# A graph network's count products: some of them moved from the tail into the gather phase

## The reference

```python
def _L0_gnn_ref(feat, weight, src, dst, etypes):
    h_src = feat[src]
    for r in range(num_rels):
        mask = etypes == r
        msg = msg + h_src * mask[:, None].astype(feat.dtype) @ weight[r]
    return jax.ops.segment_sum(msg, dst, num_segments=feat.shape[0])

def _L1_gnn_ref(x, edge_index, edge_attr, W_l, b_l, W_r, W_e, b_e):
    agg = jax.ops.segment_sum(x[row], col, num_segments=N)
    cnt = jax.ops.segment_sum(jnp.ones(...), col, num_segments=N)
    mean = agg / jnp.maximum(cnt, 1.0)[:, None]
    out = mean @ W_l + b_l + x @ W_r
    e = edge_attr @ W_e + b_e
    return out + jnp.zeros_like(out).at[col].set(e)

h = jnp.maximum(_layernorm(x), 0.0)
x = x + _L0_gnn_ref(h, L0_gnn_weight, src, dst, edge_type_16)
h = jnp.maximum(_layernorm(x), 0.0)
x = x + _L1_gnn_ref(h, edge_index, edge_attr_16, ...)
```

## Time and profile before

| | |
|---|---|
| median of three runs | 4880.84 us |
| profiled execution | 4871.31 us, span 4869.5 us |
| mean granted clock of TensorE | 0.807 |
| busy: PE, DVE, ACT, POOL | 2981.7, 3515.4, 1431.9, 3123.5 us |
| DMA | 575.14 MB, 118 GB/s over the span |

### The profile page before, as it was taken

One profiled execution on the slowest core, in us unless ns is written; L12 is line 12 of the kernel. 1 busy time (PEld: TensorE's weight loads), 2 busy tenths in 40 slices (PEclk: granted clock), 3 DMA queues, 4 the chain that ended last, 5 costly groups with the idle time before them and its releaser, 6 DMA issues.

```text
span 4869.5 us, 76484 instructions
## 1 busy us (share of the span) xinstructions
PE 2981.7 (61%) x23324; PEld 2583.8 (53%) x23325; DVE 3515.4 (72%) x17837; ACT 1431.9 (29%) x2462; POOL 3123.5 (64%) x3190
## 2 busy tenths in 40 slices
PE   1554555555555555656565565656666666669999
PEld 0224444444444544545455555555555555559999
DVE  4656788788788878888788888878877887871012
ACT  0332333333333333333333333333333333330000
POOL 1037777777777777777777777777777777770000
PEclk9975766667777777777788788888888888889999
DMA  9862333333333232223222222222222221127999
GB/s 98 300 243 85 112 106 116 104 101 99 102 109 93 85 98 90 79 82 92 81 76 68 68 70 67 67 61 62 59 55 53 50 51 45 45 78 317 408 387 365
DMA packets 257987, 575.14 MB, mean 118 GB/s; under 512 B 117787, under 2 KB 163931, under 8 KB 235323
## 3 DMA queue, kind: packets, MB, share of 16 engines
q1 hardware_dynamic: 78182, 443.67, 23.9%
q0 software_dynamic: 101568, 105.81, 11.0%
q10 hardware_dynamic: 77842, 20.86, 3.3%
HBM read 334.10 MB, written 248.81 MB: 120 GB/s over the span
## 4 chain that ended last, share of the span: by engine, by line
POOL 61%; issue 20%; PE 13%; DMA 3%; DVE 1%; ACTq 1%; ACT 1%; POOLq 0%; DVEq 0%; SPq 0%
POOL msg L413 60%; PE ps L1040 9%; PE ps L948 2%; DMA msg<-rel_table,istage 1%; DMA edge_ends<-arena 1%; POOL wrel L650 1%; ACTq L764 1%; PE ps L421 1%; DVE onehot L1145 1%; ACT arena L802 0%; DMA arena<-in_dst 0%; DVE arena L606 0%; PE ps L1024 0%; PE ps L974 0%; PE ps L958 0%
## 5 line engine op out<-in xcount | busy, mean ns | idle before, releaser
L413 POOL DMA_INDIRECT msg<-rel_table,istage x3125 | 3060.3, 979 | 954.1 <-issue 949.5
L802 ACT CAST arena<-ps 128x784 bf16<-128x784 f32 x1568 | 1245.6, 835 | 2647.5 <-PE ps L974 2634.9
L421 PE MATMUL ps<-onehot,msg 128*81 128x128 f32 x6250 | 1134.6, 347 | 1391.5 <-DMA msg<-rel_table,istage 1203.9
L421 PEld LDWEIGHTS ps<-onehot,msg 128*81 128x81 f32 x6250 | 962.9, 198 | 1515.5 <-DMA msg<-rel_table,istage 1305.8
L1285 DVE TENSOR_SCALAR batch<-iota_h,wrel 128x196 bf16<-128x196 bf16 x4312 | 1243.3, 293 | 0.0
L1284 DVE TENSOR_SCALAR batch<-iota_h,wrel 128x128 bf16<-128x128 bf16 x4312 | 1173.6, 275 | 13.7 <-PE ps L974 13.6
L974 PE MATMUL ps<-batch 128*128 128x196 bf16 x4312 | 673.1, 299 | 172.4 <-DVE batch L1285 97.6
L439 DVE TENSOR_SCALAR onehot<-iota_w,arena 128x128 f32<-128x128 f32 x3125 | 677.5, 295 | 0.0
L974 PEld LDWEIGHTS ps<-batch 128*128 128x128 bf16 x4312 | 473.3, 119 | 280.0 <-DVE batch L1285 148.5
L1285 DVE TENSOR_SCALAR arena<-iota_h,wrel 128x196 bf16<-128x196 bf16 x1960 | 564.0, 291 | 0.0
L1284 DVE TENSOR_SCALAR arena<-iota_h,wrel 128x128 bf16<-128x128 bf16 x1960 | 532.7, 275 | 10.9 <-PE ps L974 10.0
(11 more groups left out here) (147 smaller groups left out, 1116.3 us busy)
## 6 DMA issues: line engine op xcount, KB each, us to landing
arena<-counts SPq DMA_DIRECT2D x66, 1568.0 KB, 9.5
rel_table<-arena SPq DMA_DIRECT2D x98, 512.0 KB, 3.6
msg<-rel_table,istage POOLq DMA_INDIRECT x3125
counts<-arena SPq DMA_DIRECT2D x10, 3136.0 KB, 9.8
attr<-in_edge_attr SPq DMA_DIRECT2D x125, 200.0 KB
arena<-counts SPq DMA_DIRECT2D x18, 1344.0 KB, 14.4
counts<-arena SPq DMA_DIRECT2D x8, 2688.0 KB, 9.1
counts<-arena SPq DMA_DIRECT2D x7, 2912.0 KB, 9.7
```

Source lines behind the costliest of these rows:

```text
L413: pool.indirect_dma_start(msg[:, k, 0:D], None, table, bass.IndirectOffsetOnAxis(ap=istage[:, k:k + 1].bitcast(U32), axis=0)).then_inc(got ...
L421: mm = pe.matmul(ps[0:rows, bank, 0:WIN], msg[:, k, 0:rows], onehot[:, k, :], start=(k == 0), stop=(k == K - 1))
L802: nc.scalar.copy(cblk[:, h, :, u * WU * WD:(u + 1) * WU * WD].rearrange("p t (w d) -> p w t d", d=WD), unit_cols(u).rearrange("p w (t d) - ...
```

## The change

**Products of stored counts in the gather phase.** A planner now gives each slot up to 26 count products (EACH). Besides the early ones there are 148 late ones ("mults" that are not early), 3122 matmuls: as soon as more batches of `y` are final, SP reloads pieces of up to 7 source blocks of a stored count block into six rooms, three slots ahead (`load_room`), PE multiplies them (`mult_slot`), and DVE reduces the bank and adds it to `x_sb` (`mult_result`). The rooms lie over the index arrays of the first 36 superblocks, so this starts at slot 183. The tail keeps what is left, 2366 matmuls in 106 pieces instead of 5488 in 154, in five PSUM banks.

**Units of one bank.** WU goes from 4 to 2, so a unit's two products fill one PSUM bank; three banks take turns where two pairs did, and two banks are for the count products.

**Attribute product.** ACT makes it with five activations a group (`attr_group`) instead of one tensor_tensor on DVE.

```diff
-WU = 4
+WU = 2
+WINS = 16
...
-    RUNS_AT, KEY_STEPS = 8, 9
+    RUNS_AT, KEY_STEPS = 16, 9
+    RING, UNIT_BANKS = WINS // WU, (2, 3, 4)
...
+    EACH, MOST_TILES, ROOM_TILES, STORE_SLOTS, LOAD_SLOTS = 26, 28, TB, 4, 3
+    ROOMS, ROOM_SB = 6, -(-ROOM_TILES * P // K)
+    for c in range(LAST):
+        left = EACH
+        while left:
+            if not mults or mults[-1]["at"] == mults[-1]["t1"]:
...
+                    known = sum(mid_at[n]["done"] <= c for n in range(NB)) * TB
+                    least = 3 * TB if c < SLOTS - 65 else 2 * TB if c < SLOTS - 20 else TB
+                    can = [b for b in range(HEAD_WHOLE, NT) if c >= full_at[b] + STORE_SLOTS + LOAD_SLOTS
+                           and c > mid_at[b // TB]["split"] and (b < first_early or b in early_mult)
+                           and known - done[b] >= least]
...
+            mults_at[c].append((len(mults) - 1, m["at"], m["at"] + n))
...
-        def unit_cols(u):
-
-            q = 2 + 2 * (u % 2)
-            return ps[:, q:q + 2, :].rearrange("p b (w c) -> p (b w) c", w=2)[:, :, 0:HW]
+        def unit_cols(b, u):
+            q = UNIT_BANKS[(b * UB + u) % len(UNIT_BANKS)]
+            return ps[:, q, :].rearrange("p (w c) -> p w c", w=WU)[:, :, 0:HW]
...
+            def load_room(i):
+                k, t0 = late_pieces[i]
+                b, t1 = mults[k]["b"], min(t0 + ROOM_TILES, mults[k]["t1"])
+                sp.wait_ge(cstored[b % 2], stores_of(b) + 16)
...
+                else:
+                    room_read(sp, i - ROOMS)
+                sp.dma_start(rooms[i % ROOMS][:, 0:t1 - t0, :].rearrange("p t n -> p (t n)"),
+                             counts_of(b, t0, t1)).then_inc(roomed[i % ROOMS], 16)
...
+            def attr_group(s, g):
+                if g == 0:
+                    act.wait_ge(LY[0]["attr"], (s + 1) * 16)
+                for k in range(g * G, g * G + G):
+                    mark = last[:, s:s + 1, k:k + 1].rearrange("p s k -> p (s k)")
+                    ins = nc.scalar.activation(msg[:, k, D + 1:M0], attr[:, k, :], ACT.Copy, scale=mark)
+                ins.then_inc(LY[0]["attr_used"], 1)
...
             def count_unit(b, u):
                 pe.wait_ge(FU["onehots"], b * UB + (u + 1))
-                if b >= 1 or u >= 2:
-                    pe.wait_ge(FU["out"], b * UB + (u - 1))
+                if b * UB + u >= len(UNIT_BANKS):
+                    pe.wait_ge(FU["out"], b * UB + u - len(UNIT_BANKS) + 1)
...
+            def mult_slot(c):
+                for k, ta, tb in mults_at[c]:
...
+                    for t in range(ta, tb):
+                        if m["early"]:
+                            weights = cblk[:, b % 2, t, :]
+                        else:
+                            q = (t - m["t0"]) % ROOM_TILES
+                            i = late_piece[k, t - q]
+                            if q == 0:
+                                pe.wait_ge(roomed[i % ROOMS], (i // ROOMS + 1) * 16)
+                            weights = rooms[i % ROOMS][:, q, :]
+                        mm = pe.matmul(mult_bank(k), weights, y3d[:, t, :], start=(t == m["t0"]), stop=(t == m["t1"] - 1))
...
+            def mult_result(k):
...
+                nc.vector.tensor_reduce(red2[:, i % 2], three, AX, ALU.add).then_inc(FE["parts"], 1)
...
+                nc.vector.scalar_tensor_tensor(out=xt, in0=red2[:, i % 2], scalar=inv_cnt[:, b:b + 1], in1=xt,
+                                               op0=ALU.mult, op1=ALU.add).then_inc(FE["res"], 1)
```

More of the change, by code:

```diff
@@ L106, in gnn_two_layers @@
     assert all(early[b] for b in range(first_early, NT)) and max(early) < NB
-    for b in range(first_early, NT):
-        assert full_at[b] + SPREAD + 1 < mid_at[b // TB]["pend"] and mid_at[early[b] - 1]["done"] <= full_at[b] + 1
+    EACH, MOST_TILES, ROOM_TILES, STORE_SLOTS, LOAD_SLOTS = 26, 28, TB, 4, 3
+    ROOMS, ROOM_SB = 6, -(-ROOM_TILES * P // K)
+    HEAD, HEAD_WHOLE = 5, 3
+    done = [0] * NT
+    mults = []
+    mults_at = [[] for c in range(LAST)]
+    early_mult = {}
+    for c in range(LAST):
+        left = EACH
+        while left:
+            if not mults or mults[-1]["at"] == mults[-1]["t1"]:
+                if len(mults) >= 2 and mults[-2]["end"] + 2 > c:
+                    break
+                b = first_early + len(early_mult)
+                if b < NT and c > full_at[b]:
+                    mults.append({"b": b, "t0": 0, "at": 0, "t1": early[b] * TB, "early": True})
+                    early_mult[b] = len(mults) - 1
+                else:
[4 more added lines that the diff above has]
+                           and known - done[b] >= least]
+                    if not can or not ROOM_SB * NG + LOAD_SLOTS <= c < SLOTS - AHEAD - 2:
+                        break
+                    b = max(can, key=lambda b: (min(known - done[b], MOST_TILES), -b))
+                    mults.append({"b": b, "t0": done[b], "at": done[b], "t1": min(known, done[b] + MOST_TILES),
+                                  "early": False})
+            m = mults[-1]
+            n = min(left, m["t1"] - m["at"])
+            mults_at[c].append((len(mults) - 1, m["at"], m["at"] + n))
+            left -= n
+            m["at"] += n
+            if m["at"] == m["t1"]:
+                m["end"] = c
+                done[m["b"]] = m["t1"]
@@ new lines, in gnn_two_layers @@
+    for b, k in early_mult.items():
+        assert full_at[b] < mults[k]["end"] <= full_at[b] + 6 and mults[k]["end"] + 1 < mid_at[b // TB]["pend"]
+    late_mults = [k for k, m in enumerate(mults) if not m["early"]]
+    late_pieces = [(k, t) for k in late_mults for t in range(mults[k]["t0"], mults[k]["t1"], ROOM_TILES)]
+    late_piece = {piece: i for i, piece in enumerate(late_pieces)}
+    late_load_at = [[] for c in range(SLOTS)]
+    for c in range(LAST):
+        for k, t0, t1 in mults_at[c]:
+            for t in range(t0, t1):
+                if (k, t) in late_piece:
+                    late_load_at[c - LOAD_SLOTS].append(late_piece[k, t])
@@ L110, in gnn_two_layers @@
     PIECE = NT // 2
     LATE = (NB - 1) * TB
-    HEAD = 3
-    cuts = [[c for c in (early[b] * TB, PIECE, LATE if b < HEAD else NT) if c >= early[b] * TB] for b in range(NT)]
+    cuts = [[c for c in (done[b], PIECE, LATE if b < HEAD else NT) if c >= done[b]] for b in range(NT)]
     pieces = [(b, t0, t1) for b in range(HEAD) for t0, t1 in zip(cuts[b], cuts[b][1:]) if t0 < t1]
@@ L230, in gnn_two_layers @@
         oh_lo, oh_hi = [v[:, 0:P] for v in wins], [v[:, P:P + HW] for v in wins]
+        rooms = [work[:, i * S * K + h * ROOM_TILES * P // 2:i * S * K + (h + 1) * ROOM_TILES * P // 2].bitcast(BF16)
+                 .rearrange("p (t n) -> p t n", n=P) for h in range(2) for i in range(3)]
+        red2 = wrel_flat[:, P:2 * P].rearrange("p (b d) -> p b d", b=2)
         places = [work[:, i * PIECE * P // 2:(i + 1) * PIECE * P // 2].bitcast(BF16) for i in range(WORK_PLACES)]
@@ L294, in gnn_two_layers @@
         FU = family("unit", ["onehots", "done", "out"])
-        FE = family("early", ["done", "parts"])
+        FE = family("mult", ["done", "parts", "piece", "res"])
+        roomed = [sem(f"roomed{q}") for q in range(ROOMS)]
         FT = family("tail", ["piece"])
@@ L427, in stage_group, with window_group @@
             copy(istage[:, g * G:g * G + G], slots(idx, s, g)).then_inc(ly["staged"], 1)
-        def window_group(dve, ly, rows, s, t, g):
+        def window_group(dve, ly, rows, s, t, g, attr_by_act=False):
             dve.wait_ge(ly["free"], t * NG + (g + 1))
-            if rows > D:
+            if rows > D and not attr_by_act:
                 if g == 0:
@@ L1029, in tail_matmul @@
             def tail_matmul(i, t):
                 b, t0, t1 = pieces[i]
[L1031 to L1032 removed]
+                if t == done[b]:
                     pe.wait_ge(FU["out"], NT * UB)
[L1034 to L1035 removed]
+                    pe.wait_ge(s_add, added(S - 1) + 1)
+                    if b >= len(TAIL_BANKS):
+                        pe.wait_ge(FC["mean"], b - len(TAIL_BANKS) + 1)
```

138 lines of the change are left out of this document (82 added, 56 removed).

## The result

Four runs of the changed kernel took 4602.55 to 4621.74 us, median 4612.2; before 4876.6 in the same comparison. The ratio is 0.9459, 95% interval 0.9445 to 0.9474: 264 us faster. The profiled execution took 4602.55 us, its span 4600.7 us, with a mean granted clock of 0.822.

The account below looks back on a forecast made before the run. POOL's issue was taken to bound the gather phase, PE and DMA together the tail. Span 4869.5 - 5 - 251 + 1.2 = 4615 us, 4617 with 1.8 around it, 4622 as median; own range 4600 to 4650, widened to 4583 to 4668.

Parts of the forecast that it names:

- (1): Tail: 2366 of 5488 count matmuls stay, so the unbroken run falls from 433 to 182 us, minus 251.
- (2): Gather phase: 3122 moved matmuls hide under PE's waits, 48 us more against 114 in the heaviest stretch; cost nothing.
- (3): ACT's evictions of half units: 3136 casts at 0.48 us each, 152 us per 400 us against 130; hidden.
- (4): Attribute product on ACT: 3125 activations at 0.2 us, bringing ACT to about 220 of 400 us; hidden.
- (5): DVE's port shared with POOL: gathers shorten without DVE's attribute product, minus 5 us, ends 0 and minus 15.
- (6): SP's room loads: at worst 14 of 20 us lead eaten, DMA share about 0.5; cost nothing.
- PE alone in the tail: Rival: DMA keeps up in the tail and the port gives all it can, 4606 us; chance 9%.
- Hand-over too often: Rival: two-matmul units double PE's waits on ACT's evictions in the gather phase, 4652 or 4777 us; chance 8%.
- Half clock: Rival: PE's granted clock at 0.5 throughout, POOL starves in the gather phase, about 5098 us; chance 3%.
- Loads one by one: Rival: the tail's pieces do not overlap, 400 us in place of 182, total 4840 us; chance 2%.

Follow-up runs that it names:

- x7: Every late product multiplied twice into its bank, against the changed kernel: 4601.7 us, ratio 0.9444 to the kernel before.
- x11: Attribute product on ACT done in two halves of 8 columns, against the changed kernel: 4609.0 us, ratio 0.9467 to the kernel before.
- x8: Every late product multiplied four times, against the changed kernel: 4749.0 us, ratio 0.9744 to the kernel before.
- x9: Changed kernel with every tail piece after the first seven loading only its first two blocks, all products kept: 4590.1 us, one run.
- x10: Changed kernel with about every second tail product behind the head left out, all loads kept: 4619.3 us, one run.
- x3: Kernel before with only the attribute product moved to ACT, DVE's one-hot order shifted with it: 4855.9 us, ratio 0.9972 to the kernel before.
- x4: Changed kernel with the attribute product back on DVE as five tensor_tensor operations a group: 4633.8 us, ratio 0.9512 to the kernel before.
- x12: Changed kernel with room loads queued one slot ahead of use instead of three: 4606.7 us, ratio 0.9472 to the kernel before.
- x1: Changed kernel run again without an edit: 4616.1 us, ratio 0.9464 to the kernel before.
- x2: Changed kernel with the attribute product back on DVE as one tensor_tensor a group: 4621.5 us, ratio 0.9483 to the kernel before.

## Why the prediction was right, point by point

**What bounds it.** Right. POOL's own issue sets the gather phase: x7 and x11 put work on PE and ACT without moving it, and x8 shows it past the point where PE sets it.

**(1) The tail.** Right, in the sum and in its price. The run was forecast at 182 us, as 70.4 MB at 387 GB/s with PE at 176 us under it. It took 182.3 at 387 GB/s, PE alone takes 176.8 (x9), and DMA with half of the products 178.6 (x10). What the single figure hides: the run starts on seven small places at 310 GB/s, with a wait of 2.3 us for a load at 4430, and goes on at 399, with peaks of 413 to 417. That one 40 us window before had just the mean of the whole run after is in part luck; the whole run before moved 397 GB/s. The range's end of 203 us, for slow small pieces, had no ground. The Trainium skill, "DMA: Bandwidth & Descriptors", section "Anatomy of one DMA — SWDGE (gpsimd) path", has a fixed cost of about 2 us for each DMA that GpSimd issues. The estimate from it, with one DMA after the other, was about 350 us; these are issued by SP with several in flight, and the measured 182 decides.

**(2) The products in the gather phase.** Right, with some more room than I gave it. Forecast for 4000 to 4390 us: 48 us more work, 66 us of waits left. The changed kernel has 1290 products there, not 1316, and waits of 83 us ahead of the groups' products; as its last gather starts at 4375.5, 7 of them are the wait at the seam:

```profile
L1127 PE MATMUL ps<-arena 128*128 128x192 bf16 x1290 | 124.5, 256 | 0.0
```

```profile
PE ps L485 <- DMA msg<-rel_table,istage: 79.6, 31, 7.1
...
PE ps L1069 <- ACT arena L884: 14.9, 42, 0.8
...
PE ps L485 <- issue: 3.7, 4, 1.4
```

124.5 against 84.1 us is 40 us more, 0.0965 us each. The clock rose from 0.84 to 0.89 between 4000 and 4400 us, and the other work got cheaper as well: over the whole span line 485 is busy 1083.5 us, where line 421 was 1134.6.

**(3), (4) ACT.** Right. An eviction of 392 columns is 511 ns, not 480, an activation 222 ns of busy time, not 200; ACT is busy 206 of 400 us, not 220, since evictions in a row overlap (five in 2.07 us at 3807 us).

**(5) The port.** The term was mis-sized: minus 5 with an end at minus 15, measured 14 (8 to 19) by x3. Charging line 434 by its share of DVE's time was the error: by the profiles some 17 us of the excess over the median go with it, not 3.5. The Trainium skill's "SBUF — State Buffer", section "Who interferes with whom", infers that a tensor_tensor does not keep GpSimd from writing descriptors. The runs do not bear that out to the last 0.3%: with the product on DVE the gathers up to 2 us are longer. As x3 also moved DVE's timing, the port itself is argued and not shown. The memset of the earlier trace rows was no single case: in 13 of the 14 profiles 6 to 12 of the 13 memsets of 0.81 us ran beside a gather of 1.3 us or more (12 of them in the kernel before), where about one gather in 50 is that long. x4 is the exception, with none. These rows do not agree with the Trainium skill's rule, as I wrote they did: the same section holds that a DVE instruction with at most one SBUF input does not contend with GpSimd outside the 2-port modes, and the longer gathers beside a memset do not fit that.

**(6) SP.** Right that it costs nothing. The 14 us of lead that I let SP's waits eat in the worst case were not eaten: PE waited 3.9 us for rooms in x12, and not at all in the changed kernel, whose lead stayed at 19. The DMA share between 4000 and 4400 us was forecast to go from 0.23 to about 0.5 and went to 0.35, as only some 450 of the 1290 products there are late ones and need a load.

**The sum.** 4615 us of span were forecast for the profiled execution, and it had 4600.7. Of these 14 us, 11 lie in the gathers: the last one starts 16.4 us earlier than before, not 5, though the first starts 3.7 us later. The gathers themselves take 20 us less in all (3060.3 to 3040.3), 7 of which are in those over 2 us, 13 before and 4 after, and are the luck of a run, as x1's phase of 4092 us shows; 13 are in the others, of the size that x3 has for the attribute product and (5) had at 5. The other 3 lie behind the last gather, 225.2 us where the terms gave 228. The median, 4612.2, lies 10 us under 4622, and x1's, 4616.1, 6 under.

**The rivals.** PE alone in the tail: no, DMA is as full, and x9 shows that it would have given 5.5 us, where 6 were set. Hand-over too often: PE's waits for evictions are 120 us in the whole span, and were 128. Half clock: no, the mean clock rose from 0.807 to 0.822. The forecast says that only products behind a long idle stretch run at half speed; in the kernel before, the window from 400 us has a mean clock of 0.68, and a group's products take the same 2.42 us, at a granted clock of 0.50, after a wait of only 1.97 us (at 544.7 us). Loads one by one: no, the run took 182 us and not 400.

## What to carry to other kernels

When a stage is paced by one engine's issue, price what you move into it by the waits of the engine that gets it, stretch by stretch, and test the margin by doing the moved work twice and then four times: here twice was free, and four times cost 148 us. Where two limits lie on top of each other, as PE and DMA in this tail, only work that leaves both shortens it; moving a product took its load along and so did. And where single runs of a kernel differ by 10 to 40 us, read small terms from many runs, or from the profiles with the rare long instructions set apart, and not from the totals of two profiles.

## What the runs showed of the hardware that I had not expected

- A few indirect DMAs on POOL take 2 to 9.3 us where the median is 0.945 us (maximum 3492 ns in the profile before, 4537, 8528, 8720, 8942 and 9314 in later ones). Beyond 945 ns each, those over 2 us take 62 us in x1 and 11 in the first profile of the same kernel; the shorter ones gave 13 back, and the two gather phases are 37 us apart. Around three of x1's longest, at 467.7, 1296.8 and 4385.3 us, DVE was building one-hots, and the DMA share was 0.08, 0.03 and 0.58, so that full DMA engines are not what they have in common. Nor are they wholly random: the 531st gather is over 2 us in 8 of the 14 profiles, and takes 5.43 or 5.44 us in four of them and 3.63 or 3.64 in two. The very first gather takes 4.28 to 4.29 us in all eleven profiles with the attribute product on ACT, 1.23 in the kernel before, 2.86 in x2 and 1.16 in x4. The cause is open.
- Loads of 0.69 MB on average, with rows of 1.8 to 9 KB and seven places, ran at 387 GB/s over the whole run and at 399 behind its first 26 us, with 412 to 417 in single windows; the longer pieces before, 66 of them of 1568 KB, moved 397 over their run. So the smaller pieces cost at most the start.
- The granted clock of TensorE followed its load across these kernels between 3600 and 4000 us: 0.91, 0.96 and 0.99 for 294, 330 and 372 us of 400, so that added work there was partly paid for by the faster clock.
